# Grouped-query scores on TensorE row groups, and one maximum and one difference per batch

## The reference

```
Q = (x @ Wq.T).reshape(B, S, HKV, G, HEAD_DIM)      # HKV = 4, G = 4, HEAD_DIM = 16
K = (x @ Wk.T).reshape(B, S, HKV, HEAD_DIM)
V = (x @ Wv.T).reshape(B, S, HKV, HEAD_DIM)
scores = jnp.einsum('bskgd,bswkd->bskgw', Q, K_win) * scale
attn = jax.nn.softmax(scores, axis=-1)
out = jnp.einsum('bskgw,bswkd->bskgd', attn, V_win)
return out.reshape(B, S, HQ * HEAD_DIM) @ Wo.T
```

## Time and profile before

| | us |
|---|---|
| median of 3 runs | 1910.83 |
| lowest and highest | 1910.26 to 1918.58 |
| the profiled execution's own time | 1909.23 |
| its span, first to last instruction | 1907.4 |

### The profile page before, as it was taken

How to read it: one execution, slowest core, us unless ns; L and a number is a source line. 1 busy time by engine, 2 the same in 40 slices (tenths; PEclk the granted TensorE clock), 3 DMA queues, 4 the chain that set the end, 5 groups by cost and what they waited for, 6 DMA issues and landing times.

```text
span 1907.4 us, 22855 instructions
## 1 busy us (share of the span) xinstructions
PE 1664.2 (87%) x8082; PEld 1171.1 (61%) x8082; DVE 795.9 (42%) x1719; ACT 490.3 (26%) x946; POOL 387.6 (20%) x407
## 2 busy tenths in 40 slices
PE   5875998986199999999914999999899989998999
PEld 4532455546199999999912555776764446666544
DVE  3522887774011111111126661121355656675455
ACT  1234544433011111111102413123210025453000
POOL 0364776661500000000052000000010012232000
PEclk8989999995599999999966989999789999998899
DMA  7333555540525544313120000010000010000000
GB/s 255 91 91 107 146 145 129 137 112 27 215 90 191 187 148 168 135 48 133 37 82 18 1 0 28 1 45 1 1 1 1 1 44 2 1 1 1 11 17 19
DMA packets 68535, 136.68 MB, mean 72 GB/s; under 512 B 11411, under 2 KB 49204, under 8 KB 61876
## 3 DMA queue, kind: packets, MB, share of 16 engines
q1 hardware_dynamic: 65156, 126.30, 20.9%
q0 software_dynamic: 3264, 8.92, 1.4%
HBM read 196.25 MB, written 17.57 MB: 112 GB/s over the span
## 4 chain that ended last, share of the span: by engine, by line
PE 76%; DVE 9%; issue 5%; POOL 3%; SPq 3%; ACT 2%; DMA 2%; DVEq 0%; ACTq 0%; POOLq 0%
PE psum L688 40%; PE psum L969 13%; PE psum L720 8%; PE psum L783 4%; PE psum L899 2%; PE psum L698 2%; PE psum L894 1%; DVE work L1749 1%; SPq L587 1%; DVE work L1748 1%; ACT work L1069 1%; PE psum L954 1%; POOL xn L1819 1%; PE psum L978 1%; POOL work L1859 1%
## 5 line engine op out<-in xcount | busy, mean ns | idle before, releaser
L688 PE MATMUL psum<-work 128*128 128x128 f32 (+4 forms) x3528 | 479.3, 297 | 15.4 <-DMA work<-in_xp 15.4
L688 PEld LDWEIGHTS psum<-work 128*128 128x128 f32 (+1 forms) x3528 | 449.2, 191 | 33.4 <-DMA work<-in_xp 15.4
L969 PE MATMUL psum<-w_late,xn 128*128 128x512 f32 x544 | 243.1, 605 | 0.0
L1673 DVE TENSOR_TENSOR work<-sq,psum 128x512 f32<-128x512 f32 x82 | 56.3, 687 | 428.8 <-PE psum L688 428.8
L969 PEld LDWEIGHTS psum<-w_late,xn 128*128 128x128 f32 x544 | 104.0, 194 | 129.2 <-issue 119.7
L1606 DVE TENSOR_TENSOR_SCAN work<-psum,work 128x414 f32<-128x414 f32 (+1 forms) x160 | 160.4, 1060 | 49.5 <-POOL work L1841 26.2
L1841 POOL TENSOR_TENSOR work<-work 128x408 f32<-128x408 f32 (+1 forms) x160 | 161.8, 1040 | 65.4 <-PE psum L783 52.6
L1069 ACT ACTIVATE work<-psum 68x364 f32<-68x364 f32 (+10 forms) x266 | 113.6, 467 | 198.5 <-PE psum L688 66.9
L1490 DVE SCALAR_TENSOR_TENSOR h<-psum,gate,h 128x256 f32<-128x256 f32 x272 | 119.3, 479 | 107.9 <-PE psum L969 104.8
L1800 POOL TENSOR_TENSOR rs<-rs,power 128x4 f32<-128x4 f32 (+3 forms) x40 | 44.6, 1116 | 565.1 <-DVE rs L1337 550.0
L783 PE MATMUL psum<-work,xn 128*128 128x408 f32 (+1 forms) x320 | 134.2, 555 | 14.1 <-POOL work L1841 14.0
(11 more groups left out here) (235 smaller groups left out, 1979.9 us busy)
## 6 DMA issues: line engine op xcount, KB each, us to landing
work<-in_W SPq DMA_DIRECT2D x123, 1024.0 KB
work<-c_rows SPq DMA_DIRECT2D x48, 204.0 KB, 4.0
w_attn<-in_B SPq DMA_DIRECT2D x64, 128.0 KB, 2.5
w_attn<-in_A SPq DMA_DIRECT2D x64, 128.0 KB, 2.7
work<-c_rows SPq DMA_DIRECT2D x32, 238.0 KB, 4.1
x_slots<-work SPq DMA_DIRECT2D x1, 5248.0 KB, 28.1
work<-x_slots SPq DMA_DIRECT2D x41, 128.0 KB, 4.5
y_slots<-sq SPq DMA_DIRECT2D x41, 128.0 KB, 4.3
```

Source lines behind the costliest of these rows:

```text
L688: mm = pe.matmul(dst, lhs(k), rhs(k), start=(k == 0), stop=(k == parts - 1))
L969: mm = pe.matmul(dst.rearrange("p (e n) -> p e n", e=2), xn[:, k, i * P:(i + 1) * P], w_last[:, 2 * q:2 * q + 2, k, :], start=(k == 0), st ...
L1673: dve.tensor_tensor(hm[:, j % 2, 4 * q:4 * q + 4, :].rearrange("p k n -> p (k n)"), sa[:, i % 2], A.at(("e3", j, q)), ALU.mult).then_inc(s ...
```

## The change

- The scores of a batch are computed one key head at a time: 3 pieces x 4 heads = 12 matmuls of 32 contraction rows (`tile_position=(g * HPAD, 0)`) and 68 columns. Head g writes bank g, the three pieces beside one another in it. One semaphore count stands for the whole batch.
- VectorE takes the maximum of all 816 columns of a batch in one operation over four banks, and the difference in one more.
- The keys are kept as they come, in one ScalarE copy for a chunk; the block diagonal matrix and the GpSimd clearing of it are gone.
- Since a batch's scores fill four banks, the rings are cut anew: `S4`, banks 0 to 3, for the scores, and `T`, banks 4 and 5, for all that ran through `A` in this attention: keys, values, queries, the three banks of `pT3` and `out3`. The layer norm of the following layer (`L3F`) uses `T` too.

```diff
-        kblk = carve(KR * KV_HEADS * SEQ).rearrange("p (b g s) -> p b g s", g=KV_HEADS, s=SEQ)
+        k3 = carve(KR * SEQ).rearrange("p (b s) -> p b s", s=SEQ)
...
+        S4 = Banks(psum, [0, 1, 2, 3], tenants)
+        T = Banks(psum, [4, 5], tenants)
...
-        ln_ring = {L0A: F, L3A: W8}
+        ln_ring = {L0A: F, L3A: W8, L3F: T}
...
         def plan_s3(b):
-            for i in range(PIECES):
-                A.plan(("s3", b, i), (sem("s3_shifted"), PIECES * b + i + 1))
+            for g in range(KV_HEADS):
+                S4.plan(("s3", b, g), (sem("s3_shifted"), b + 1))
             step("s3", b)
...
                 for i in range(PIECES):
-                    A.plan(("pT3", b, i), (sem("pT3_kept"), PIECES * b + i + 1))
+                    T.plan(("pT3", b, i), (sem("pT3_kept"), PIECES * b + i + 1))
...
-                plan_h("out3", L3A, c)
+                plan_h("out3", L3A, c, T)
...
+                banks = [S4.wait_free(pe, ("s3", b, g)) for g in range(KV_HEADS)]
                 for i in range(PIECES):
-                    dst = A.wait_free(pe, ("s3", b, i))
-                    pe.matmul(dst[0:PROWS, 0:KV_HEADS * SEQ],
-                              q3[:, c % 2, b - CHUNK_B0[c], PIECE0[i]:PIECE0[i] + PROWS], kblk[:, at3(b)],
-                              start=True, stop=True).then_inc(sem("s3_done"), 1)
+                    for g in range(KV_HEADS):
+                        rows = slice(g * HPAD, (g + 1) * HPAD)
+                        mm = pe.matmul(banks[g][0:PROWS, i * SEQ:(i + 1) * SEQ],
+                                       q3[rows, c % 2, b - CHUNK_B0[c], PIECE0[i]:PIECE0[i] + PROWS], k3[rows, at3(b), :],
+                                       start=True, stop=True, tile_position=(g * HPAD, 0))
+                mm.then_inc(sem("s3_done"), 1)
...
-                src = A.at(("k3", c))
-                for g in range(KV_HEADS):
-                    rows = slice(g * HPAD, (g + 1) * HPAD)
-                    ins = act.activation(kblk[rows, at3(CHUNK_B0[c]):at3(CHUNK_B0[c]) + CHUNK_BATCHES[c], g, :],
-                                         seqs(src[rows, 0:ntok(c)]), ACT.Copy)
-                ins.then_inc(sem("k3_kept"), 1)
+                copy(k3[:, at3(CHUNK_B0[c]):at3(CHUNK_B0[c]) + CHUNK_BATCHES[c], :], seqs(T.at(("k3", c))[:, 0:ntok(c)]), "k3_kept")
...
             def shift3(b):
-                for i in range(PIECES):
-                    dve.wait_ge(sem("s3_done"), PIECES * b + i + 1)
-                    s = A.at(("s3", b, i))[0:PROWS, 0:KV_HEADS * SEQ].rearrange("p (g s) -> p g s", g=KV_HEADS)
-                    mx = st3[0:PROWS, b % (AHEAD + 1), 0, i * KV_HEADS:(i + 1) * KV_HEADS]
-                    link(dve.tensor_reduce(mx, s, AX_X, ALU.max))
-                    dve.tensor_tensor(p3[0:PROWS, b % (AHEAD + 1), i], s,
-                                      mx.unsqueeze(2).to_broadcast([PROWS, KV_HEADS, SEQ]),
-                                      ALU.subtract).then_inc(sem("s3_shifted"), 1)
+                dve.wait_ge(sem("s3_done"), b + 1)
+                s = psum[0:PROWS, S4.bank["s3", b, 0]:S4.bank["s3", b, 0] + KV_HEADS, 0:PIECES * SEQ].rearrange(
+                    "p g (i s) -> p i g s", i=PIECES)
+                mx = st3[0:PROWS, b % (AHEAD + 1), 0, :].rearrange("p (i g) -> p i g", i=PIECES)
+                link(dve.tensor_reduce(mx, s, AX_X, ALU.max))
+                dve.tensor_tensor(p3[0:PROWS, b % (AHEAD + 1)], s,
+                                  mx.unsqueeze(3).to_broadcast([PROWS, PIECES, KV_HEADS, SEQ]),
+                                  ALU.subtract).then_inc(sem("s3_shifted"), 1)
...
-            wait_all(pool, L2F)
-            pool.memset(kblk, 0.0).then_inc(sem("pool_setup"), 1)
```

More of the change, by code:

```diff
@@ L498, in plan_qkv3 @@
         def plan_qkv3(c):
-            A.plan(("k3", c), (sem("k3_kept"), c + 1))
+            T.plan(("k3", c), (sem("k3_kept"), c + 1))
             for j in range(V3[c]):
-                A.plan(("v3", c, j), (sem("v3_kept"), V30[c] + j + 1))
+                T.plan(("v3", c, j), (sem("v3_kept"), V30[c] + j + 1))
             step("kv3", c)
             for j in range(GROUP):
-                A.plan(("q3", c, j), (sem("q3_kept"), GROUP * c + j + 1))
+                T.plan(("q3", c, j), (sem("q3_kept"), GROUP * c + j + 1))
             step("q3", c)
         def plan_s3(b):
-            for i in range(PIECES):
-                A.plan(("s3", b, i), (sem("s3_shifted"), PIECES * b + i + 1))
+            for g in range(KV_HEADS):
+                S4.plan(("s3", b, g), (sem("s3_shifted"), b + 1))
             step("s3", b)
@@ L985, in kv3 @@
                 wait_normed(pe, L3A, c)
-                dst = A.wait_free(pe, ("k3", c))
+                dst = T.wait_free(pe, ("k3", c))
                 product(dst[:, 0:ntok(c)], lambda k: wk3[:, k, :], lambda k: xn[:, k, chunk(c)],
@@ L989, in kv3 @@
                 for j in range(V3[c]):
-                    dst = A.wait_free(pe, ("v3", c, j))
+                    dst = T.wait_free(pe, ("v3", c, j))
                     for i in range(4 * j, min(4 * j + 4, CHUNK_BATCHES[c])):
@@ L998, in q3_ @@
                 for j in range(GROUP):
-                    dst = A.wait_free(pe, ("q3", c, j))
+                    dst = T.wait_free(pe, ("q3", c, j))
                     product(dst[:, 0:ntok(c)], lambda k: wq3[:, k, j, :], lambda k: xn[:, k, chunk(c)],
@@ L1015, in pT3_ @@
                 for i in range(PIECES):
-                    dst = A.wait_free(pe, ("pT3", b, i))
+                    dst = T.wait_free(pe, ("pT3", b, i))
                     for g in range(KV_HEADS):
@@ L1033, in out3 @@
                 pe.wait_ge(sem("o3_kept"), CHUNK_B0[c] + CHUNK_BATCHES[c])
-                into_h("out3", wo3, lambda k, cols: oT3[:, k, cols], c, GROUP)
+                into_h("out3", wo3, lambda k, cols: oT3[:, k, cols], c, GROUP, T)
             steps = {"ln": ln, "hT": hT, "tok": tok, "prims": prims, "guards": guards, "z": z, "dt": dt, "yacc": yacc,
@@ L1265, in keep_kv3 @@
                     act.wait_ge(sem("v3_done"), V30[c] + j + 1)
-                    copy(vb3[0:SEQ, at3(b):at3(b) + n, :], A.at(("v3", c, j))[0:SEQ, 0:n * P].rearrange("p (b n) -> p b n", n=P),
+                    copy(vb3[0:SEQ, at3(b):at3(b) + n, :], T.at(("v3", c, j))[0:SEQ, 0:n * P].rearrange("p (b n) -> p b n", n=P),
                          "v3_kept")
@@ L1272, in keep_q3 @@
                     if c >= 2 and j == 0:
-                        act.wait_ge(sem("s3_done"), PIECES * CHUNK_B0[c - 1])
-                    copy(q3[:, c % 2, 0:CHUNK_BATCHES[c], j * SEQ:(j + 1) * SEQ], seqs(A.at(("q3", c, j))[:, 0:ntok(c)]),
+                        act.wait_ge(sem("s3_done"), CHUNK_B0[c - 1])
+                    copy(q3[:, c % 2, 0:CHUNK_BATCHES[c], j * SEQ:(j + 1) * SEQ], seqs(T.at(("q3", c, j))[:, 0:ntok(c)]),
                          "q3_kept")
             def exp3(b):
-                act.wait_ge(sem("s3_shifted"), PIECES * (b + 1))
+                act.wait_ge(sem("s3_shifted"), b + 1)
                 v = p3[0:PROWS, b % (AHEAD + 1)]
@@ L1304, in _ @@
                     copy(pT3[0:SEQ, :, PIECE0[i] - lap:PIECE0[i] + PROWS],
-                         A.at(("pT3", b, i))[0:SEQ, 0:KV_HEADS * PROWS].rearrange("p (g q) -> p g q",
+                         T.at(("pT3", b, i))[0:SEQ, 0:KV_HEADS * PROWS].rearrange("p (g q) -> p g q",
                                                                                  g=KV_HEADS)[:, :, -lap:PROWS],
@@ L1769, in _ @@
                 if b and (b == BATCH or b in CHUNK_B0):
-                    add_h(L3A, "out3", CHUNKS - 1 if b == BATCH else CHUNK_B0.index(b) - 1)
+                    add_h(L3A, "out3", CHUNKS - 1 if b == BATCH else CHUNK_B0.index(b) - 1, T)
             router(2)
```

3 lines of the change are left out of this document (1 added, 2 removed).

## The result

| | before | after |
|---|---|---|
| median, us | 1914.7 (4 runs, 1910.26 to 1920.06) | 1969.5 (4 runs, 1964.09 to 1976.8) |
| ratio | | 1.0287, 95% interval 1.0239 to 1.0336 |
| profiled execution: time, span | 1909.23, 1907.4 | 1976.8, 1975.0 |
| stage: first score matmul to the end of the last `out3` | 1559.5 to 1755.7: 196.2 | 1566.3 to 1822.3: 256.1 |
| one chunk of six batches, `kv3` to `kv3` | 37.5 | 49.6 and 50.4 |

The account below looks back on a forecast made before the run. VectorE was taken to set 3.6 us a batch between projections, and the two-bank ring to bind after the change. 1909.2 + 32 (ring, including 5 outside the full stretches) + 18 (clock) = 1959 us, range 1932 to 1990.

Parts of the forecast that it names:

- The circle: Two-bank ring `T`: third transpose bank waits for ScalarE's same-batch copy, closing a loop; 4.95 us a batch against 3.60, +32.
- The scores: A batch's 24 score instructions on TensorE: 0.70 us taken, 0.5 to 2.0 kept as bounds.
- rival 3: Row groups run one after another: scores of 1.2 to 2.0 us, 1957 to 1979 at the high clock; chance 0.20.
- The clock: TensorE's waits in each round lower its clock to 1.2 GHz: 31 us if all is low, about 18 taken.
- The term that was too small: Lone rounds in the first and last chunks and first batches behind projections: 5 us more.
- VectorE's part: One long maximum and one difference a batch on VectorE: 2.04 us where 2.40 was needed, a gain of 0.4.
- Rival 4: VectorE's shorter batch sets the pace, not the ring: 3.2 us a batch, 9 us faster, 1900 us; chance 0.05.

## Why the prediction was right

- **The circle.** Forecast 4.95 us a round at the high clock, measured 4.87 where the clock was held. The rings alone, put into the kernel before, cost as much as the whole change, and a third bank takes 35 to 40 us back. This step is shown.
- **The scores.** Forecast 0.70 us for 24 instructions, measured 0.71. Row groups overlap, as the column groups of the earlier trace rows do; the bound of 2.0 us from the earlier trace rows, for groups one after another, does not hold for them, and rival 3 with it. The figure of the Trainium skill ("TensorE: Matmul & The Clock Gate", Part 3), 3.07 times the speed for four row tiles of 512 columns, had given an estimate of 0.65.
- **The clock.** It fell, as in the earlier trace rows. Its 18 us came out near the 19 by which the stage shortens when the waits are filled, but by two errors against each other. I took 18 of 31 us, on the ground that the projections warm TensorE anew. They do, but the first long wait behind them, 2.31 us, already loses the clock, and nearly all later rounds run at 0.50, so the share was too small. A round at the low clock was sized too long: 0.95 us more were forecast, 0.80 measured. That the sum fits is in part luck.
- **The term that was too small** is the one for all that is not a round inside a chunk. The stage grew by 59.9 us in the profiled executions, where 50 were forecast. By the times between exponentials, the 20 rounds inside the last four chunks grew by 41.6 us: 25.7 with the clock held (27 forecast for the circle) and 16.0 for the clock. The other 11 intervals, at the start of the stage, around the projections and in the last batches, grew by 16.8 us, where 5 were forecast beside a share of the clock; with the waits filled they still grew by 15.2 us, what the filling costs there included. One part of it can be seen at the start: scores of a new batch wait until VectorE has let go of all four banks, so the second exponential follows the first after 3.18 us in place of 2.46.
- **VectorE's part.** Forecast 2.04 us for maximum and difference, measured 2.07 in the circle and 1.97 without pauses (1599.91 to 1601.88).
- **Rival 4** (VectorE's shorter batch decides) gave 3.2 us a round and 1900 us. The kernel in which the ring does not bind and the clock is held runs at 3.18 and takes 1900.1. It was the right price for a case that the changed kernel is not in. One condition was missing from it: without the circle, but with nothing else done, the clock still falls in most chunks, and it is 1927 us.

## What to carry to other kernels

When PSUM banks are dealt out anew, ask for each product which copy frees its bank, and whether that copy waits, through the orders of the engines, for something queued behind the product. If it does, the latencies of all engines in that circle add up, and a faster operation gives back only its own part of the sum: VectorE's 0.3 to 0.4 us a batch here, against 2.07 us that the rounds grew by. A faster matmul in a pipeline that another engine paces also takes work away from TensorE; when the granted clock falls, TensorE can become the bound with less to do, so look at the granted clock of the rounds and not only at their busy time.

## What the runs showed of the hardware that I had not expected

- TensorE can lose the clock with no waits longer than 0.74 us. In the kernel with a third bank and scores first it fell to half speed in three of four chunks after one, two and four rounds of 3.2 us, and stayed at 1.00 through the fourth, in rounds of the same work; over 120 us the timeline shows TensorE busy for 108.5 at a mean granted clock of 0.83. With scores on full rows (1.38 us a round) or 0.65 us of added 128-row matmuls it stayed at 1.00 in every chunk. What decides between the two levels is not shown.
- Once at the low clock the rounds of these kernels stay there: in the kernel with a third bank, rounds of 4.16 to 4.6 us with waits of at most 0.37 us did not bring it back; the output matmuls and projections behind them did.
- A maximum over 816 columns in four PSUM banks takes 1.00 us (1004 ns on average), where a sum over 816 columns from SBUF takes 0.99 (986 ns); reading across banks costs next to nothing here.
